# A graph network's edge sorting: paired one-hots, a maximum in pieces, ranks by column, and x transposed later

## The chip, the cores and the metric

One core of one Trainium2 chip runs the kernel as one program. The time is in device microseconds (us), the median of several executions. The engines are PE (TensorE, its weight loads shown apart as PEld), DVE (VectorE), ACT (ScalarE), POOL (GpSimd) and SP (SyncE, which here only starts DMAs). SBUF is the memory beside the engines, PSUM the one that PE writes.

## What is computed

A graph network with 3 layers on 3125 nodes of 128 features and 100,000 edges with 16 features each:

```python
s2 = concatenate([src, dst]); d2 = concatenate([dst, src]); ef2 = concatenate([ef, ef], axis=0)
h_prev = nf
for l in range(3):
    e_in = concatenate([h_prev[s2], h_prev[d2], ef2], axis=-1)
    msg = leaky_relu(e_in @ We1[l]) @ We2[l]
    red = segment_sum(msg, d2, num_segments=N)
    out = leaky_relu(concatenate([h_prev, red], axis=-1) @ Wn1[l]) @ Wn2[l]
    h_prev = out + h_prev
# result: _layernorm(x + out)
```

## The kernel before, in words

Nodes lie in 25 blocks of 128 (`NB`). An edge goes into one of 650 buckets by the blocks of its lower and its higher end, and a bucket's edges fill whole tiles of 128, so that in the layers every gather and every sum of a tile is a product with a one-hot matrix against one block. The kernel first sorts the edges into `records` in DRAM (up to about 1140 us), then builds tables and reads the records back (to about 1220 us), then runs the three layers. The change lies in the first two.

The 128 x 784 edges are worked on by column: 28 groups (`GROUPS`) of 28 columns (`GROUP`), each group in 4 chains of 7 columns (`CHAINS`, `RUN`).

- **Preparation** (DVE, L893 to L913). When all seven constants and both edge lists have landed: lower and higher end (L896, L897), their block numbers `lo_b` and `hi_b` (L898, L899), the places inside the block with a mark for padding, `loc` (L900 to L905), `ident16`, `zeros`, `ones`, and the bucket number `key` with two f16 copies (L911 to L913). PE transposes these (L1300), ACT copies them out (L739), and SP writes them to `rows_d` (L513), from where they come back as rows spread over all partitions, `hrow` and `krow` (L523, L528).
- **Counting** (DVE L940 and L927, PE L1311 and L1313, ACT L746). For each group DVE makes one-hots of the higher block (128 x 896, f16) and of the lower block (128 x 700, f16), comparing int32 block numbers with `iota`. PE multiplies them, once for each of 7 steps into one of two banks that ACT copies out to `cols` in four instructions of 32 partitions, and once more to add them up in `gath`.
- **Maximum** (DVE L945). The greatest absolute edge feature, one reduction over 128 x 12544; POOL then takes it across partitions (L658), and a scale of the features follows (L972 to L975).
- **First slots** (DVE L950 to L969). Totals, bucket sizes by a product on PE (L1330, L1332), tile numbers by a scan. Beside the maximum, PE transposes x (L1322) and ACT copies it to `hT` (L754).
- **The loop over groups** (DVE L1004 to L1059). `chain_bases` (L978 to L998) makes the starts of each bucket for a group; PE takes them to the edges (L1340). DVE then ranks each edge among the 128 of its column: equality of `krow` with the key (L1017), times a triangle of ones in PSUM, `tri_ps` (L1020), summed (L1023, into `within`). L1026 and L1032 pick the base, L1039 to L1053 make the record's row number `rowi`, L1056 the low half of the record, and `rec_set` is raised. Before the ranks of a group, `chain_bases` of the next one is done. `rec` and `rowi` are double: `rowi` of a group waits for the scatters of the group two before, `moved[h]`.
- **Scatter** (POOL L673). For each of the 28 columns of a group, one indirect DMA puts 128 records into place, 784 in all. Before the first, POOL waits until the whole of `records` is filled with blanks: two small DMAs of its own (L662) and two large ones of SP (L507), which repeat a block `blank` of 8 records of 68 bytes per partition, 544 bytes in one run.
- **Behind the loop** DVE finds out which tile belongs to which bucket (L1061 to L1090), clears buffers (L1091 to L1095), takes the maximum of `hT` (L1098), absolute weights (L1101), norms and scales (L1105 to L1122); PE and ACT make the first tables (L1353, L804) from `hT`; then PE transposes the records read back (L1407).

All of it runs on five queues in the written order; semaphores are the only ties between them. Inside the ranking and `chain_bases` several operands had been copied to PSUM beforehand (L758 to L761, L771), so that those DVE instructions have only one tensor in SBUF.

## Time and profile before

| | us |
|---|---|
| median of 3 executions | 3580.88 |
| lowest, highest | 3576.39, 3668.85 |
| the profiled execution | 3580.29 |
| its span in the profile | 3578.6 |
| POOL busy with scatters | 751.5 |
| DVE busy | 2741.3 (77%) |
| PE busy | 2436.7 (68%) |

The span reaches from the first to the last instruction that the profile shows; the profiled execution's own time lies 1.7 us above it. Times in the rows are counted from the span's start. The busy share of an engine says little here: the sorting at the beginning and the layers behind it have different limits.

### The profile page before, as it was taken

Reading aid. Unit: us, or ns where it says so; the run is one execution under the profiler, and the core shown is the slowest. Engines: PE = TensorE matmul, PEld = TensorE weight load, DVE = VectorE, ACT = ScalarE, POOL = GpSimd, SP = SyncE. Lnnn points to the kernel's source line nnn. Section 1 sums busy time; section 2 is a strip of 40 time slices with the busy share of each in tenths; the row PEclk is TensorE's granted clock in tenths of the full one; section 3 lists DMA queues with packets and bytes.
Section 4 is the critical chain, followed back from the end, with each engine's and each line's share of the span. In section 5 each row is a group of like instructions: output and inputs, shape, how many; then the busy total and the mean of one; then the engine's idle time right before and its main releaser. Section 6 shows DMA issues by size and latency. Waiting matters only on the chain.

```text
span 3578.6 us, 80654 instructions
## 1 busy us (share of the span) xinstructions
PE 2436.7 (68%) x26761; PEld 2103.2 (59%) x26762; DVE 2741.3 (77%) x3385; ACT 2062.6 (58%) x4138; POOL 800.0 (22%) x870
## 2 busy tenths in 40 slices
PE   5000000000004899999999999999999999999996
PEld 4000000000003678788787788888888788888885
DVE  8956565656564799999999877777777777777776
ACT  4000000000001678788777688888888688888885
POOL 0477777777775100000000100000000100000000
PEclk9555555555556899999999999999999999999998
DMA  8111111111112777777777455555555355555553
GB/s 251 46 45 33 45 37 41 34 44 37 39 22 71 234 257 248 253 254 250 248 257 246 174 193 192 193 192 194 195 195 195 107 195 195 195 193 193 191 193 123
DMA packets 227347, 563.67 MB, mean 158 GB/s; under 512 B 43272, under 2 KB 124238, under 8 KB 227182
## 3 DMA queue, kind: packets, MB, share of 16 engines
q1 hardware_dynamic: 199758, 547.80, 44.7%
q0 software_dynamic: 27552, 15.37, 2.3%
q8 instruction: 24, 0.39, 0.0%
q14 instruction: 13, 0.11, 0.0%
HBM read 413.11 MB, written 150.16 MB: 157 GB/s over the span
## 4 chain that ended last, share of the span: by engine, by line
PE 50%; POOL 19%; DVE 15%; issue 13%; DMA 1%; SPq 1%; ACT 1%; DVEq 0%; another core or an unknown queue 0%; ACTq 0%; POOLq 0%
POOL records L673 19%; PE gath L1454 18%; PE sums L1516 14%; PE sums L1454 9%; PE gath L1447 5%; DVE loop_buf L1200 3%; DVE big L1180 3%; PE sums L1447 2%; DVE loop_buf L1217 2%; DVE gsel L1184 2%; DVE table L1138 1%; DVE table L927 1%; PE sums L1537 1%; PE sums L1538 1%; DVE gsel L1064 0%
## 5 line engine op out<-in xcount | busy, mean ns | idle before, releaser
L1180 DVE SCALAR_TENSOR_TENSOR big<-big 128x768 f32<-128x768 f32 (+1 forms) x957 | 908.2, 949 | 360.2 <-ACT big L843 333.9
L1454 PE MATMUL gath<-table,gsel 128*128 x7488 | 1073.6, 273 | 0.0
L1200 DVE TENSOR_TENSOR loop_buf<-big,loop_buf 128x768 f16<-128x768 f32 x936 | 889.9, 951 | 0.0
L673 POOL DMA_INDIRECT records<-rec,rowi x784 | 751.5, 959 | 284.5 <-issue 247.3
L1516 PE MATMUL sums<-loop_buf 128*128 128x128 f16 x11232 | 781.2, 219 | 18.7 <-issue 15.8
L1454 PEld LDWEIGHTS gath<-table,gsel 128*128 128x128 f16 x7488 | 733.1, 98 | 84.0
L847 ACT ACTIVATE loop_buf<-big 128x768 f16<-128x768 f32 x936 | 782.4, 836 | 0.0
L843 ACT ACTIVATE big<-gath 128x512 f32<-128x512 f32 x936 | 560.0, 598 | 269.7 <-PE gath L1454 269.7
L1516 PEld LDWEIGHTS sums<-loop_buf 128*128 128x128 f16 x11232 | 647.0, 98 | 113.8 <-ACT sums L841 38.9
L1340 PE MATMUL sums<-table,fchunk 128*128 128x200 f16 x196 | 37.1, 365 | 877.2 <-DVE found L1032 864.7
L1454 PE MATMUL sums<-table,gsel 128*128 x3744 | 562.4, 273 | 14.6 <-DVE gsel L1184 14.6
L1340 PEld LDWEIGHTS sums<-table,fchunk 128*128 128x128 f16 x196 | 24.7, 136 | 889.3 <-issue 886.9
L783 ACT ACTIVATE rec<-big,sc_ef 128x448 f16 x28 | 18.7, 668 | 881.1 <-DMA records<-rec,rowi 881.1
L1447 PE MATMUL gath<-wst,fchunk 128*128 128x256 f16 x1872 | 510.9, 273 | 0.0
L838 ACT ACTIVATE big<-sums 128x256 f32<-128x256 f32 x936 | 353.4, 378 | 75.5 <-PE sums L1454 73.2
L1454 PEld LDWEIGHTS sums<-table,gsel 128*128 128x128 f16 x3744 | 361.2, 98 | 60.4 <-DVE gsel L1184 28.9
L841 ACT ACTIVATE sums<-iota 128x256 f32<-128x256 f16 x936 | 362.9, 388 | 30.3
L708 POOL TENSOR_SCALAR wcs<-wts,sc_w 128x128 f32<-128x128 f32 x2 | 1.2, 611 | 1573.1 <-DVE sc_w L1122 1573.1
L1447 PE MATMUL sums<-wst,fchunk 128*128 128x256 f16 x936 | 255.6, 273 | 21.0 <-issue 21.0
L1053 DVE SCALAR_TENSOR_TENSOR rowi<-rowb,rowc 128x28 int32<-128x28 int32 x28 | 5.3, 188 | 326.3 <-DMA records<-rec,rowi 326.0
L1447 PEld LDWEIGHTS gath<-wst,fchunk 128*128 128x128 f16 x1872 | 183.0, 98 | 31.7
L1217 DVE TENSOR_TENSOR loop_buf<-numc,iota 128x768 f16<-128x768 f16 x312 | 171.9, 551 | 3.9 <-DMA ssel_d<-loop_buf 0.3
(196 smaller groups left out, 1655.6 us busy)
## 6 DMA issues: line engine op xcount, KB each, us to landing
gsel<-gsel_d SPq DMA_DIRECT2D x208, 576.0 KB, 3.7
loop_buf<-ssel_d SPq DMA_DIRECT2D x208, 576.0 KB, 5.1
numb<-nums_d SPq DMA_DIRECT2D x106, 576.0 KB, 4.7
gsel_d<-gsel SPq DMA_DIRECT2D x104, 576.0 KB, 5.5
ssel_d<-loop_buf SPq DMA_DIRECT2D x104, 576.0 KB, 6.5
fchunk<-feat_d SPq DMA_DIRECT2D x630, 80.0 KB, 4.5
loop_buf<-rows_d SPq DMA_DIRECT2D x28, 896.0 KB
records<-rec,rowi POOLq DMA_INDIRECT x784
```

Source lines behind the costliest of these rows:

```text
L673: pool.indirect_dma_start(out=records[:, :], out_offset=bass.IndirectOffsetOnAxis(ap=rowi[:, h, g:g + 1].bitcast(U32), axis=0), in_=rec[:, ...
L838: act.activation(msg[:, place, 0:2 * D], gath6, ACT.Copy).then_inc(x6_set, 1)
L841: act.activation(gath6, iota[:, 0:2 * D], ACT.Copy, scale=0.0).then_inc(gath6_free, 1)
L843: act.activation(msg[:, place, 2 * D:MSG], gath[:, :], ACT.Copy).then_inc(x_set, 1)
L847: act.activation(m_hi[:, (q - 1) % RING, :], msg[:, (q - 1) % RING, :], ACT.Copy)\
L1180: return dve.scalar_tensor_tensor(m, m, SLOPE, m, ALU.mult, ALU.max)
L1184: dve.tensor_scalar(gsel[:, h, :], numb[:, h, :], part[:, 0:1], None, ALU.is_equal).then_inc(gsel_set[h], DMA)
L1200: dve.tensor_tensor(m_lo[:, place, :], msg[:, place, :], m_hi[:, place, :], ALU.subtract)\
L1217: last = dve.tensor_tensor(ssel[:, t % SLOTS:t % SLOTS + STEP, :, :].rearrange("p t s (e w) -> p (t s) e w", w=2), numc[:, 2 * t:2 * (t + ...
L1447: pe.matmul(uv, fchunk[:, p % PARTS, pair * P:(pair + 1) * P], wst[:, side, :, :].rearrange("p s f -> p (s f)"), start=fresh, stop=False, ...
L1454: return pe.matmul(uv, gsel[:, h, (2 * tc + s) * P:(2 * tc + s + 1) * P], at[n], start=False, stop=n == 3, skip_group_check=True)
L1516: last = pe.matmul(sum_at[i, s], m[:, place, w0:w0 + D], ssel[:, ts, s, :], start=False, stop=False, skip_group_check=True)
```

## The change

- **Order of loads.** The edge lists are loaded before the constants; DVE waits for the constants only behind `key`.
- **Preparation.** The ends, the shifts and `key` stay on DVE (5 instructions). POOL makes `zeros`, `ones` and `loc`, the latter in nine instructions on 784 elements each; ACT makes `ident16`, the f16 copies, and `lo_pairs` and `hi_pairs`, the block numbers as f16, each written twice side by side, `hi_pairs` with its columns in the order in which PE takes them.
- **Counting.** Both one-hots compare such pairs with pairs of `iota`; the lower one is made 26 wide (728 elements). PE reads its operands with strides accordingly.
- **Maximum.** It is taken in 16 pieces of 784 elements, one behind each of the last 16 groups' one-hots; across partitions by a product of `ones` with a scaled identity on PE and a reduction, in place of POOL's instruction.
- **Ranks.** `count_within` works on one column at a time: one instruction compares 128 elements of `krow` with a key per partition, multiplies by the triangle and accumulates; 28 of them per group. The triangle is now read from SBUF (`tri`), and the key is a scalar in SBUF; the output goes over `krow` as before.
- **Order in the loop.** The bases and ranks of the first group are made ahead of the loop, those of each next group behind `rec_set` of the one before.
- **x.** SP loads it when the last ranks are done (`krow_free`), PE transposes it behind the last `rec_set`, in four banks in turn, and ACT copies it to `hT`. DVE waits for PE (`hT_ps`) before it clears `loop_buf`, and for ACT (`hT_in`) before L1098.
- **Rows.** `load_rows` starts a group's four loads of `hrow` and its one of `krow` together; the first two groups' come ahead of SP's loop, the others when both buffers are free.
- **Blanks.** `blank` lies in a part of `recc` and has 64 records per partition; SP's blanking DMAs write runs of 3264 and 4352 bytes and come behind the rows of the first two groups.

```diff
+        hi_pairs, lo_pairs = (words_at(COLS, 2 * GROUP * NB + GROUP * NB + k * COLS).bitcast(F16).rearrange("p (j w) -> p j w", w=2)
+                              for k in range(2))
...
+        blank = recc[:, 2:4, :, :, :].rearrange("p k h t f -> p (k h t) f")
...
-            sp.dma_start(x0, x.rearrange("(b p) f -> p b f", p=P)).then_inc(s_x, 16)
-            sp.wait_ge(blank_set, 2)
-            for c0, c1 in ((2, CHUNKS // 2), (CHUNKS // 2, CHUNKS)):
-                sp.dma_start(records[c0 * CHUNK * P:c1 * CHUNK * P, :].rearrange("(c p t) f -> p c (t f)", p=P, t=CHUNK),
-                             blank[:, :, :].rearrange("p t f -> p (t f)").unsqueeze(1)
-                             .to_broadcast([P, c1 - c0, CHUNK * RW])).then_inc(blanked, 16)
...
+            for h in range(2):
+                load_rows(h * GROUP, h)
+            sp.wait_ge(blank_set, 2)
+            for r0, t, c in ((2 * CHUNK, 6 * CHUNK, 1), (8 * CHUNK, 8 * CHUNK, TILES // (8 * CHUNK) - 1)):
+                sp.dma_start(records[r0 * P:(r0 + t * c) * P, :].rearrange("(c p t) f -> p c (t f)", p=P, t=t),
+                             blank[:, 0:t, :].rearrange("p t f -> p (t f)").unsqueeze(1)
+                             .to_broadcast([P, c, t * RW])).then_inc(blanked, 16)
+            with sp.Fori(1, GTURNS) as it:
                 for h in range(2):
                     sp.wait_ge(hrow_free, it * 2 + h - 1 + KROW_AHEAD)
                     sp.wait_ge(krow_free, it * 2 + h - 1 + KROW_AHEAD)
                     sp.sem_inc(sp_go, 1)
-
+                    load_rows((it * 2 + h) * GROUP, h)
+
+            sp.wait_ge(krow_free, GROUPS + KROW_AHEAD)
+            sp.dma_start(x0, x.rearrange("(b p) f -> p b f", p=P)).then_inc(s_x, 16)
...
+            pool.memset(zeros[:, :], 0.0).then_inc(consts_set, 1)
+            pool.memset(ones[:, :], 1.0).then_inc(consts_set, 1)
+
+            pool.wait_ge(dve_seq, SHIFT_STEP)
+            for s, numbers in enumerate((lo_n, hi_n)):
+                pool.tensor_scalar(loc[:, :, s], numbers[:, :], 1.0, None, ALU.mult).then_inc(loc_seq, 1)
+            for s, blocks in enumerate((lo_b, hi_b)):
+                pool.wait_ge(loc_seq, 2 + 2 * s)
+                pool.tensor_scalar(dead, blocks, float(-P), None, ALU.mult).then_inc(loc_seq, 1)
+                pool.wait_ge(loc_seq, 3 + 2 * s)
+                pool.tensor_tensor(loc[:, :, s], loc[:, :, s], dead, ALU.add).then_inc(loc_seq, 1)
+            pool.wait_ge(loc_seq, 6)
+            pool.tensor_scalar(dead, hi_b, float(NB), float(-DEAD), ALU.is_equal, ALU.mult).then_inc(loc_seq, 1)
+            pool.wait_ge(loc_seq, 7)
+            for s in range(2):
+                pool.tensor_tensor(loc[:, :, s], loc[:, :, s], dead, ALU.add).then_inc(loc_seq, 1)
...
-            pool.partition_all_reduce(efmax[:, 1:2], efmax[:, 0:1], P, bass.bass_isa.ReduceOp.max).then_inc(efmax_all, 1)
...
+            act.wait_ge(s_const, 16 * 7)
+            act.activation(ident16[:, :], ident[:, :], ACT.Copy).then_inc(key16_set, 1)
+            act.wait_ge(dve_seq, SHIFT_STEP - 1)
+            act.activation(lo_pairs, lo_b.unsqueeze(2).to_broadcast([P, COLS, 2]), ACT.Copy).then_inc(pairs_set, 1)
+            act.wait_ge(dve_seq, SHIFT_STEP)
+            for r in range(CHAINS):
+                act.activation(hi_pairs.rearrange("p (g q r) w -> p r g q w", q=RUN, r=CHAINS)[:, r],
+                               hi_b.rearrange("p (g r q) -> p r g q", r=CHAINS, q=RUN)[:, r].unsqueeze(3)
+                               .to_broadcast([P, GROUPS, RUN, 2]), ACT.Copy).then_inc(pairs_set, 1)
+            act.activation(hib16, hi_b, ACT.Copy).then_inc(key16_set, 1)
+            act.wait_ge(dve_seq, KEY_STEP)
+            act.activation(key16, key[:, :], ACT.Copy).then_inc(key16_set, 1)
+            act.wait_ge(loc_seq, 2)
...
-            dve.wait_ge(s_const, 16 * 7)
             dve.wait_ge(s_edges, 32)
             then(dve.tensor_tensor(lo_n[:, :], src_t[:, :], dst_t[:, :], ALU.min))
             then(dve.tensor_tensor(hi_n[:, :], src_t[:, :], dst_t[:, :], ALU.max))
             then(dve.tensor_scalar(lo_b, lo_n[:, :], 7, None, ALU.logical_shift_right))
             then(dve.tensor_scalar(hi_b, hi_n[:, :], 7, None, ALU.logical_shift_right))
-            then(dve.tensor_scalar(src_t[:, :], lo_n[:, :], P - 1, None, ALU.bitwise_and))
-            then(dve.tensor_scalar(dst_t[:, :], hi_n[:, :], P - 1, None, ALU.bitwise_and))
-
-            then(dve.tensor_scalar(key[:, :], hi_b, float(NB), float(-DEAD), ALU.is_equal, ALU.mult))
-            then(dve.tensor_tensor(loc[:, :, 0], src_t[:, :], key[:, :], ALU.add))
-            then(dve.tensor_tensor(loc[:, :, 1], dst_t[:, :], key[:, :], ALU.add))
-            then(dve.tensor_copy(ident16[:, :], ident[:, :]))
-            then(dve.memset(zeros[:, :], 0.0))
-            then(dve.memset(ones[:, :], 1.0))
-            assert steps[0] == LOC_STEP
-
+            assert steps[0] == SHIFT_STEP
             then(dve.scalar_tensor_tensor(key[:, :], hi_b, float(NB), lo_b, ALU.mult, ALU.add))
-            then(dve.tensor_copy(key16, key[:, :]))
-            then(dve.tensor_copy(hib16, hi_b))
             assert steps[0] == KEY_STEP
+            dve.wait_ge(s_const, 16 * 7)
...
+            def hot_pairs(out, pairs, group, width):
+
+                dims = [P, GROUP, width // 2, 2]
+                return dve.tensor_tensor(out.rearrange("p j (a w) -> p j a w", w=2),
+                                         pairs[:, ds(group * GROUP, GROUP), :].unsqueeze(2).to_broadcast(dims),
+                                         iota[:, 0:width].rearrange("p (a w) -> p a w", w=2).unsqueeze(1).to_broadcast(dims),
+                                         ALU.is_equal)
+
+            dve.wait_ge(pairs_set, 1 + CHAINS)
+            def hot_group(group, h):
+
+                dve.wait_ge(hist_done, group - 1 + HIST_AHEAD)
+                hot_pairs(hot_hi[:, h, :, :], hi_pairs, group, HW)
+                hot_pairs(hot_lo[:, h, :, :], lo_pairs, group, LW).then_inc(hist_hot_set, 1)
+
+            with dve.Fori(0, GTURNS - EF // 2) as it:
                 for h in range(2):
-
-                    dve.wait_ge(hist_done, it * 2 + h - 1 + HIST_AHEAD)
-                    dve.tensor_tensor(hot_hi[:, h, :, :].rearrange("p q (r a) -> p q r a", a=HW), by_run(hi_b, it * 2 + h, HW),
-                                      numbers(HW), ALU.is_equal)
-                    hot_lo_of(hot_lo[:, h, :, :], it * 2 + h).then_inc(hist_hot_set, 1)
-
+                    hot_group(it * 2 + h, h)
             dve.wait_ge(s_ef, 16)
-            dve.tensor_reduce(efmax[:, 0:1], ef_t, AX_X, ALU.max, apply_absolute_value=True).then_inc(efmax_ready, 1)
+            with dve.Fori(GTURNS - EF // 2, GTURNS) as it:
+                for h in range(2):
+                    hot_group(it * 2 + h, h)
+                    f = nc.s_assert_within(it * 2 + (h - 2 * GTURNS + EF), 0, EF - 1,
+                                           skip_runtime_bounds_check_because="the last EF groups")
+                    dve.tensor_reduce(ef_most[:, ds(f, 1)], ef_t[:, ds(f * COLS, COLS)], AX_X, ALU.max,
+                                      apply_absolute_value=True)
...
+            def count_within(group, turn, h):
+
+                dve.tensor_copy(keyg, key[:, ds(group * GROUP, GROUP)]).then_inc(keyg_set, 1)
+                dve.wait_ge(krow_in[h], turn * 16 + 16)
+                dve.wait_ge(keyg_set, group + 1)
+                for j in range(GROUP):
+                    keys = krow[:, h, j * P:(j + 1) * P]
+                    last = dve.scalar_tensor_tensor(keys, keys, keyg[:, j:j + 1], tri[:, 1, :], ALU.is_equal, ALU.mult,
+                                                    accum_out=within[:, j:j + 1])
+                last.then_inc(krow_free, 1)
+
+            count_within(0, 0, 0)
+            dve.wait_ge(consts_set, 2)
+            dve.tensor_reduce(efmax[:, 0:1], ef_most[:, :], AX_X, ALU.max).then_inc(efmax_ready, 1)
+            dve.wait_ge(efmax_ready, 1)
+            dve.tensor_scalar(wcs[:, :], ident[:, :], efmax[:, 0:1], None, ALU.mult).then_inc(efd_set, 1)
...
+            then(dve.tensor_reduce(efmax[:, 1:2], bank(6)[:, 0:P], AX_X, ALU.max))
...
-                    keys = krow[:, h, :].rearrange("p (j e) -> p j e", e=P)
-                    dve.wait_ge(krow_in[h], it * 16 + 16)
-                    dve.tensor_tensor(keys, keys, key_ps[:, ds(group * GROUP, GROUP)].unsqueeze(2).to_broadcast([P, GROUP, P]),
-                                      ALU.is_equal).then_inc(same_set, 1)
-                    dve.wait_ge(same_set, group + 1)
-                    dve.tensor_tensor(keys, keys, tri_ps.unsqueeze(1).to_broadcast([P, GROUP, P]), ALU.mult)\
-                       .then_inc(before_set, 1)
-                    dve.wait_ge(before_set, group + 1)
-                    dve.tensor_reduce(within[:, :], keys, AX_X, ALU.add).then_inc(krow_free, 1)
...
+                    if h == 0:
+                        chain_bases(it * 2 + 1, it, 1)
+                        count_within(it * 2 + 1, it, 1)
+                    else:
+                        with dve.If(it < GTURNS - 1):
+                            after = nc.s_assert_within(it + 1, 1, GTURNS - 1,
+                                                       skip_runtime_bounds_check_because="not the last turn")
+                            chain_bases(after * 2, after, 0)
+                            count_within(after * 2, after, 0)
...
-            pe.wait_ge(s_x, 16)
             pe.wait_ge(cols_set, GROUPS + COLS_AHEAD)
             pe.wait_ge(rowsT_set, 1)
-            pe.sem_inc(pe_go, 1)
-            for b in range(NB):
-                last = pe.transpose(sums[:, b * P:(b + 1) * P], x0[:, b, :], ident[:, :])
-                if b % 4 == 3 or b == NB - 1:
-                    last.then_inc(hT_ps, 1)
-
-            pe.wait_ge(hT_in, BANKS)
...
+            pe.wait_ge(efd_set, 1)
+            pe.matmul(bank(6)[:, 0:P], ones[:, :], wcs[:, :], start=True, stop=True).then_inc(efmax_all, 1)
...
+            pe.wait_ge(s_x, 16)
+            pe.sem_inc(pe_go, 1)
+            for n in range(BANKS):
+                if n >= XT_BANKS:
+                    pe.wait_ge(hT_in, n + 1 - XT_BANKS)
+                for b in range(4 * n, min(4 * n + 4, NB)):
+                    last = pe.transpose(xT_bank(n)[:, b % 4 * P:(b % 4 + 1) * P], x0[:, b, :], ident[:, :])
+                last.then_inc(hT_ps, 1)
```

## Rows read from the trace of the kernel before

**Rows 1.** Groups of POOL: count, busy us, mean ns, idle us before, releasers.

```profile
L673 POOL DMA_INDIRECT records<-rec,rowi x784 | 751.5, 959 | 284.5 <-issue 247.3 <-DVE rec L1056 37.1
...
L716 POOL TENSOR_TENSOR wst<-wcs,wch 32x256 f16<-32x256 f32 x4 | 2.7, 668 | 0.3
...
L708 POOL TENSOR_SCALAR wcs<-wts,sc_w 128x128 f32<-128x128 f32 x2 | 1.2, 611 | 1573.1 <-DVE sc_w L1122 1573.1
```

**Rows 2.** Timeline of DVE inside the scatters: start us, us, instruction, idle before.

```profile
394.83 0.27 DVE L1039 SCALAR_TENSOR_TENSOR slot_i<-found,within 128x28 int32<-128x28 f32 x1
...
432.12 0.19 DVE L1048 SCALAR_TENSOR_TENSOR rowc<-rowa,slot_i 128x28 int32<-128x28 int32 x1
444.99 0.19 DVE L1053 SCALAR_TENSOR_TENSOR rowi<-rowb,rowc 128x28 int32<-128x28 int32 x1 [12.68 <-DMA records<-rec,rowi]
```

**Rows 3.** Timeline of DVE at the end of the scatters.

```profile
1051.61 0.19 DVE L1053 SCALAR_TENSOR_TENSOR rowi<-rowb,rowc 128x28 int32<-128x28 int32 x1 [17.37 <-DMA records<-rec,rowi]
...
1054.67 0.89 DVE L1064 SCALAR_TENSOR_TENSOR gsel<-sums,tiles_c,loop_buf 128x650 f32<-128x650 f32 x1
...
1055.61 0.89 DVE L1064 SCALAR_TENSOR_TENSOR gsel<-sums,tiles_c,loop_buf 128x650 f32<-128x650 f32 x1
...
1095.75 3.49 DVE L1098 TENSOR_REDUCE mx<-hT 128x1 f32<-128x3200 f32 x1
1099.15 1.75 DVE L1101 SCALAR_TENSOR_TENSOR big<-wts 128x1536 f32<-128x1536 f32 x1
1100.82 0.28 DVE L1103 TENSOR_SCALAR big<-ident,mx 128x128 f32<-128x128 f32 x1
```

**Rows 4.** Timeline of ACT and PE behind the last scatter.

```profile
1129.23 2.42 ACT L804 ACTIVATE table<-sums,sc 128x512 f16<-128x512 f32 x4 [7.73 <-remote]
...
1141.99 1.25 PE L1407 MATMUL sums<-ident,recc 128*68 128x128 f16 x10 [5.07 <-issue]
```

**Rows 5.** Timeline of DVE up to the first scatter.

```profile
10.52 0.97 DVE L896 TENSOR_TENSOR table<-table 128x784 int32<-128x784 int32 x1 [10.52 <-DMA below<-c_below]
...
21.78 1.09 DVE L940 TENSOR_TENSOR table<-table,iota 128x896 f16<-128x896 f16 x1
...
23.59 1.09 DVE L940 TENSOR_TENSOR table<-table,iota 128x896 f16<-128x896 f16 x1
...
72.19 13.21 DVE L945 TENSOR_REDUCE efmax<-big 128x1 f32<-128x12544 f32 x1
...
89.90 0.90 DVE L960 TENSOR_SCALAR table<-sums 128x325 int32<-128x325 f32 x2 [2.90 <-PE sums L1332]
...
102.07 0.57 DVE L982 TENSOR_TENSOR_SCAN sums<-gath,numb 128x200 f32<-128x200 f32 x1
...
106.75 3.88 DVE L1017 TENSOR_TENSOR loop_buf<-loop_buf,sums 128x3584 f16<-128x3584 f16 x1
```

**Rows 6.** Timeline of ACT at the start of the counting.

```profile
22.92 1.73 ACT L739 ACTIVATE fchunk<-sums 112x896 f16<-112x896 f16 x2 [20.17 <-PE sums L1300]
...
27.04 1.26 ACT L746 ACTIVATE table<-sums 32x175 f32 x4 [0.53 <-PE gath L1313]
```

**Rows 7.** One of the page's costliest groups: a one-hot of the first layer.

```profile
L1217 DVE TENSOR_TENSOR loop_buf<-numc,iota 128x768 f16<-128x768 f16 x312 | 171.9, 551 | 3.9 <-DMA ssel_d<-loop_buf 0.3
```

**Rows 8.** Timeline of POOL: the first scatter, and three near the end.

```profile
124.38 1.08 POOL L673 DMA_INDIRECT records<-rec,rowi  x1 [37.15 <-DVE rec L1056]
...
1098.77 0.96 POOL L673 DMA_INDIRECT records<-rec,rowi  x1 [0.30 <-issue]
1100.03 1.70 POOL L673 DMA_INDIRECT records<-rec,rowi  x1 [0.31 <-issue]
```

**Rows 9.** Timeline of PE: the first product of the bases.

```profile
102.30 1.32 PE L1340 MATMUL sums<-table,fchunk 128*128 128x200 f16 x7 [12.44 <-DVE table L994]
```

**Rows 10.** DMA issues up to 130 us: issues, KB each, median us to landing.

```profile
big<-ef SPq DMA_DIRECT2D x1, 6272.0 KB, 20.3
...
records<-blank SPq DMA_DIRECT2D x1, 4760.0 KB, 41.2
```

More of the change, by code:

```diff
@@ L257, in build @@
         rec = sb("rec", [P, 2, GROUP, RW], F16)
-        blank = sb("blank", [P, CHUNK, RW], F16)
         recc = sb("recc", [P, SLOTS_IN, PREP, CHUNK, RW], F16)
         hrow = recc[:, :, :, :, :].rearrange("p k h t f -> p (k h t f)")[:, 0:2 * RUN * P].rearrange("p (h e) -> p h e", h=2)
+        ef_most = sb("ef_most", [P, EF], F32)
+        blank = recc[:, 2:4, :, :, :].rearrange("p k h t f -> p (k h t) f")
+        assert SLOTS_IN == 4 and 2 * RUN * P <= 2 * BATCH * RW // P * P
         num16 = sb("num16", [P, 2, 2 * BATCH], F16)
@@ L357, in build @@
         consts_ps = sem("consts_ps")
-        key_in_ps = sem("key_in_ps")
+        pairs_set = sem("pairs_set")
+        consts_set = sem("consts_set")
+        key16_set = sem("key16_set")
+        loc_seq = sem("loc_seq")
+        efd_set = sem("efd_set")
+        keyg_set = sem("keyg_set")
         rec_set = sem("rec_set")
@@ L736, in _ @@
             act.sem_inc(cols_set, COLS_AHEAD)
+            act.wait_ge(s_const, 16 * 7)
[3 more added lines that the diff above has]
+            act.wait_ge(dve_seq, SHIFT_STEP)
+            for r in range(CHAINS):
+                act.activation(hi_pairs.rearrange("p (g q r) w -> p r g q w", q=RUN, r=CHAINS)[:, r],
[5 more added lines that the diff above has]
+            act.wait_ge(loc_seq, 2)
             act.wait_ge(rowsT_ps, 1)
@@ L750, in _ @@
                     last.then_inc(cols_set, 1)
-            for n in range(BANKS):
-                w = WIDE[n][1]
-                act.wait_ge(hT_ps, n + 1)
-                act.activation(hT[:, n * BANK:n * BANK + w], sums[:, n * BANK:n * BANK + w], ACT.Copy).then_inc(hT_in, 1)
             act.wait_ge(expand_set, 1)
@@ L769, in _ @@
                 line_of(h, h)
[L770 to L771 removed]
             act.wait_ge(scef_ready, 1)
[L773 removed]
+            act.wait_ge(loc_seq, 9)
             with act.Fori(0, GTURNS) as it:
@@ L804, in tables @@
                     act.activation(ab_table(s, 0), ab_bank(s), ACT.Copy, scale=sc[:, 0:1]).then_inc(thi_set, 1)
+            for n in range(BANKS):
+                w = WIDE[n][1]
+                act.wait_ge(hT_ps, n + 1)
+                act.activation(hT[:, n * BANK:n * BANK + w], xT_bank(n)[:, 0:w], ACT.Copy).then_inc(hT_in, 1)
             act.wait_ge(w2t_ps, 1)
@@ L1006, in _ @@
                     group = it * 2 + h
-                    if h == 0:
-                        chain_bases(it * 2 + 1, it, 1)
-                    else:
-                        with dve.If(it < GTURNS - 1):
-                            after = nc.s_assert_within(it + 1, 1, GTURNS - 1,
-                                                       skip_runtime_bounds_check_because="not the last turn")
-                            chain_bases(after * 2, after, 0)
-                    keys = krow[:, h, :].rearrange("p (j e) -> p j e", e=P)
-                    dve.wait_ge(krow_in[h], it * 16 + 16)
-                    dve.tensor_tensor(keys, keys, key_ps[:, ds(group * GROUP, GROUP)].unsqueeze(2).to_broadcast([P, GROUP, P]),
-                                      ALU.is_equal).then_inc(same_set, 1)
-                    dve.wait_ge(same_set, group + 1)
-                    dve.tensor_tensor(keys, keys, tri_ps.unsqueeze(1).to_broadcast([P, GROUP, P]), ALU.mult)\
-                       .then_inc(before_set, 1)
-                    dve.wait_ge(before_set, group + 1)
-                    dve.tensor_reduce(within[:, :], keys, AX_X, ALU.add).then_inc(krow_free, 1)
                     dve.wait_ge(base_ps, group + 1)
@@ L1294, in _ @@
             pe.sem_inc(hist_done, HIST_AHEAD)
-            pe.wait_ge(s_const, 16 * 7)
-            pe.wait_ge(dve_seq, KEY_STEP)
-            pe.sem_inc(pe_go, 1)
-            for k, numbers in ((0, key16), (1, hib16)):
+            pe.wait_ge(consts_set, 2)
+            for k, numbers in ((1, hib16), (0, key16)):
+                pe.wait_ge(key16_set, 3 - k)
+                pe.sem_inc(pe_go, 1)
                 for t in range(ROW_PARTS):
@@ L1365, in _ @@
             pe.wait_ge(rec_set, GROUPS + AHEAD)
+            pe.wait_ge(s_x, 16)
+            pe.sem_inc(pe_go, 1)
+            for n in range(BANKS):
+                if n >= XT_BANKS:
[3 more added lines that the diff above has]
+                last.then_inc(hT_ps, 1)
             pe.wait_ge(w_in, W_DMAS * DMA)
```

56 lines of the change are left out of this document (27 added, 29 removed).

## The prediction

> **What bounds the kernel now.** First the groups of instructions on POOL: 784 scatters of 959 ns stand in front of everything, and nearly all idle time between them is POOL's own issue, 247 us; only once, for 37.1 us, did it wait for DVE [rows 1]. Their starts lie 1.263 us apart, so 28 (a group) take 35.4 us, and the phase runs from 124.38 for 751.5 + 247.3 us to 1123.2. Then DVE's timeline inside that phase: its work for one group ends at 432.3, and its next instruction starts at 444.99, held 12.68 us by the scatters of two groups before [rows 2]. So in the loop DVE has 13 us to spare per group, and what it saves there is worth nothing; what makes POOL's scatters longer counts in full. Last, the end of the phase: the last group's index work on DVE waits for POOL at 1051.6 [rows 3], and from there a chain of tile map, norms and tables runs beside the last two groups to PE's transposes at 1141.99, 19 us after the last scatter [rows 4]. It hangs on the scatters by a fixed distance. Two things therefore move the time: when the first scatter starts (124.38), and how long 784 of them take. Everything behind 1142 is the same code, 2437 us of the 3578.6.
>
> **Part 1: up to the first scatter.** Before, DVE started at 10.52, the constants' landing, and made its first counting one-hot at 21.78 [rows 5]. Now the edges are loaded first; nine POOL instructions make `loc`, three DVE instructions of 1 us and five short ones leave DVE, and ACT fills the pairs. The constants still land at 10.5. ACT then writes 128 + 1568 + 4 x 392 elements; at the 175-element evictions' price (309 ns, four in 1.26 [rows 6]) and about 0.9 ns an element that is 0.25 + 1.5 + 2.5 = 4.3 us, so pairs stand at 15, `hib16` and `key16` (0.7 each) at 16.3. PE's 14 transposes end 1.1 behind, two copies of 1.73 together [rows 6] bring ACT to 19.4, and the first count eviction ends at 20.8, where it was 26.5 before (the second one's 27.04, less one turn of 1.80, plus 1.26).
>
> Counting: before, two DVE one-hots at 1x set a pitch of 1.81 us (21.78 to 23.59), 28 of them 50.4 us; then the feature maximum, 13.21 us in one piece [rows 5]. The paired form exists in the kernel already: 768 f16 elements in 551 ns [rows 7], which is 400 ns of stream at two elements a cycle and 151 ns around it; overlapped by 85 ns with its neighbour the pitches become 0.53 for 896 elements and 0.45 for 728, 0.98 us together. Next to it ACT's four evictions take 1.26 us and were idle 0.53 of each turn [rows 6]; with the hand-over I take 1.4 as the new pitch. A piece of the maximum is 13.21 / 16 = 0.83 plus 0.05. So 12 groups at 1.4 bring PE to 36.2 (DVE is two groups ahead, at 34.2), then 16 at 0.98 + 0.88 = 1.86 are 29.8: DVE is through at 64.0, PE at 64.7, where before the maximum ended at 85.4. If the pairs ran at 1x the pitch would stay 1.8 and 2.7 and 17 us of this part would be gone (a twentieth chance, since [rows 7] is the same form).
>
> From there to the scatter: 39.0 us before, 85.4 to 124.38 [rows 5, 8]. Gone: PE's 2.90 us wait, since the ranks of group 0 cover it, and one of the two `chain_bases` (102.07 to 106.75, 4.68). Added: 1.65 for the product of PE (1.32 busy [rows 9]), which the second `chain_bases` had hidden, and 1.2 for the maximum's reduce, scaling and read back. The ranks were 11.64 us in three passes of 3.88; now they are 28 times a 128-element pass with an accumulator. The map's 650-element ones have a pitch of 0.94 [rows 3]; less 522 elements at 1.04 ns that is 0.40, less the wait between dependent ones 0.37: 28 x 0.37 = 10.4 us, bounds 0.30 (8.4) and 0.50 (14). Sum 39.0 - 2.9 - 4.7 + 1.65 + 1.2 - 1.2 = 33.1, so the first scatter is at 64.7 + 33.1 = 97.8, 26.6 us earlier.
>
> What could be late: `loc` on POOL. A 128-element scalar op is 611 ns, a 256-element two-input op 668 ns [rows 1]: if all of it is fixed, nine ops cost 6 us, if all is per element 27; I take 18, done at 27, the 2176-element blank at 29. ACT needs `loc` only when the feature scale stands, behind 85. The blanking then starts behind the row loads, about 35; before, its second half landed 41.2 us after its issue, with the features (20.3 us) in front of it [rows 10], so 77 at the latest, now with rows eight times as long and nothing in front. POOL would have to take 6 us per op to make it the last. The pairs and POOL's ops meet for about 10 us while ACT sets the pace; I charge 3 us for it (0 to 10). Part 1: -24 us, range -29 to -10.
>
> **Part 2: the 784 scatters.** The ranks were formed with one operand in PSUM (`tri_ps`); now each of the 28 passes reads two tensors from SBUF, while POOL scatters. Of the 784 scatters only one behind the first two is above 0.98 us: the one at 1100.03 lasted 1.70 [rows 8]. Beside it DVE ran its only large instruction with two SBUF tensors, 1.75 us from 1099.15 on [rows 3]; the scatter before, begun at 1098.77, was at work when that one began and kept its 0.96 us. So a scatter that starts while such an instruction streams is held until it is over, 0.74 us here, and one that has started is not. How long POOL itself holds on: `slot_i`, 28 elements and two SBUF inputs, took 0.27 us where it started 0.03 before a scatter [rows 2], and 0.21 where it started 0.08 or more behind one. The read at a scatter's start is thus short.
>
> The Trainium skill, "SBUF — State Buffer", section "Who interferes with whom", says that a Vector instruction with two SBUF inputs contends with a GpSimd instruction that reads SBUF, and that whoever comes second is blocked for the whole of the other. The trace agrees for the scatter behind, not for the reverse: the 1.75 us instruction was as long as its elements make it although a scatter was running.
>
> Price: the passes of a group last 10.4 us, so 8.2 of its 28 scatters start among them, 221 in the 27 groups whose ranks are formed during scatters. A pass streams 0.133 us of 0.37 and lasts 0.28 at most. Held by the stream alone: 36% meet it, 0.067 mean, 5 us in all. Held for its whole duration: 76%, 0.14 mean, 24 us. I take 8, nearer to the first, since the 1.70 us scatter fits a release at the end of the stream (1100.8). Below nothing it can't be: POOL's pace never falls under 1.26 in this trace.
>
> **Part 3: moves with no price.** `chain_bases` and the ranks behind `rec_set` only change their order in DVE's 20 us, in front of 13 us of slack. x is loaded and transposed behind the last ranks: 25 transposes on PE with 7 copies on ACT beside them start at 1054, when DVE begins its map, and DVE needs `hT` at 1095.75 [rows 3]; even at 1 us a transpose they would be through at 1080. Before, they lay beside the maximum, so their leaving frees nothing by itself. SP's queue loses its first x load and gets rows earlier; its later waits are the same. The chain to 1142 keeps its length, but holds an ACT idle of 7.73 us that no engine of this core ended [rows 4]; it may fall elsewhere: 0, give or take 8.
>
> **Sum.** The profiled execution is 3580.3 us (span 3578.6), the median 3580.9. 3580.9 - 24 + 8 = 3565 us.
>
> **Rivals.** A, the other side: every scatter among the passes is held for a whole pass, or behind several. At 24 us / 221 = 0.11 us each the gain is used up; at 0.28 the loop grows by 62 us: 3580.9 - 24 + 62 = 3619. Were POOL shut out of a whole burst, 27 x 10.4 = 281 us: 3838. For it: the row of 0.74 us. Against the worst: behind the large instruction another DVE one follows at once (1100.82), and the scatter still went on.
> B: no hold at all, as a pass is short and its accumulator read leaves gaps: 3581 - 27 = 3554. For it: the map's 18 passes (one input in PSUM) lengthened no scatter.
> C: the opening gives back half: POOL's ops and the pairs shut each other out (7 us more than charged), ACT's strided copies are twice as long (2.5), a pass is 0.50 (3.6): 3565 + 13 = 3578.
> D: the pairs don't run at two elements a cycle: 12 x 1.82 + 16 x 2.70 = 65 us of DVE from 15.9 on, through at 81 instead of 64: 3565 + 17 = 3582.
>
> **How the numbers follow.** Forecast 0.60; A 0.17, of which 0.04 for bursts shut out; B 0.13; C and D 0.10. Without the worst of A and the best of B the range is 3546 to 3602. Two per cent is 72 us, about what a measurement of this kernel can tell from no change; the whole opening is 124 us and can't give 72, so faster by that 0.01, slower 0.05 (A's upper half), within 0.94.
>
> **What would show it.** Right: first scatter near 98; ACT back to back in the first 12 counting groups; one-hots of 0.61 and 0.53 us; a few scatters per group of 1.0 to 1.25 us, none outside the passes; 35.6 to 35.9 us a group. Wrong: groups of 36.5 us or more (A), 35.4 (B), `loc` or blanking released last before the first scatter (C), one-hots of 1.09 us (D), DVE no longer idle before `rowi`, or a tail behind the last scatter other than 19 us.

## The result: 3752.09 us against 3581.22, a ratio of 1.048, and the profile after

The changed kernel took 3752.09 us (four runs, 3749.01 to 3753.68), the kernel before 3581.22 beside it: a ratio of 1.048 with an interval of 1.046 to 1.050, where the forecast was 3565 and the range ended at 3602. (On chips like this one some runs of the kernel before take 3664 to 3672 us, 7 of 20 in all, where on the other kind of chip, told apart below, none of 67 was above 3576; they are left out of the ratios.) The profiled execution has a span of 3750.9 us, 172.3 more than before.

The opening went as forecast. DVE's timeline there, and POOL's first and last scatter:

```profile
13.42 1.07 DVE L969 TENSOR_TENSOR table<-table,iota 128x896 f16<-128x896 f16 x2 [3.09 <-ACT table L775]
...
59.67 0.53 DVE L969 TENSOR_TENSOR table<-table,iota 128x728 f16<-128x728 f16 x1
...
65.69 0.96 DVE L990 TENSOR_REDUCE ef_most<-big  x1
...
69.56 0.35 DVE L1011 SCALAR_TENSOR_TENSOR loop_buf<-loop_buf,gsel,tri 128x128 f16<-128x128 f16 x1 [0.54 <-DVE gsel L1006]
69.84 0.08 DVE L1011 DVE_READ_ACCUMULATOR loop_buf<-loop_buf,gsel,tri 128x1 f32 x1
69.84 0.35 DVE L1011 SCALAR_TENSOR_TENSOR loop_buf<-loop_buf,gsel,tri 128x128 f16<-128x128 f16 x1
```

One-hots of 0.53 us are the paired form at two elements a cycle, the last piece of the maximum ends at 66.65 (forecast 64.0), and the passes follow each other in steps of 0.27 us (forecast 0.37). The first scatter starts at 97.70 where 97.8 was forecast and 124.38 was before [rows 8].

The loss starts behind it. From the groups of POOL and DVE (count, busy, mean ns, idle before, releasers):

```profile
L705 POOL DMA_INDIRECT records<-rec,rowi x784 | 759.6, 969 | 477.7 <-issue 243.2 <-DVE rec L1100 234.5
```

```profile
L1011 DVE SCALAR_TENSOR_TENSOR loop_buf<-loop_buf,gsel,tri 128x128 f16<-128x128 f16 x784 | 242.9, 349 | 321.6 <-issue 314.9 <-DVE gsel L1006 4.9
...
L1011 DVE DVE_READ_ACCUMULATOR loop_buf<-loop_buf,gsel,tri 128x1 f32 x784 | 63.8, 81 | 254.4 <-issue 253.9
```

The scatters themselves take 8.1 us more than the 751.5 before [rows 1]: the forecast's part 2. But POOL now waits 234.5 us for DVE, 63.5 of it ahead of the first scatter and 171.0 in 13 waits of 12 to 14 us, one in every second group. And DVE, whose passes are busy for 243 + 64 us, stood idle for 569 us in front of them with "issue" as the reason: nothing the profile shows held it. How that looks, in DVE's timeline of one group:

```profile
463.20 0.35 DVE L1011 SCALAR_TENSOR_TENSOR loop_buf<-loop_buf,gsel,tri 128x128 f16<-128x128 f16 x1
463.47 0.08 DVE L1011 DVE_READ_ACCUMULATOR loop_buf<-loop_buf,gsel,tri 128x1 f32 x1
...
466.04 0.35 DVE L1011 SCALAR_TENSOR_TENSOR loop_buf<-loop_buf,gsel,tri 128x128 f16<-128x128 f16 x1 [1.31 <-issue]
467.44 0.08 DVE L1011 DVE_READ_ACCUMULATOR loop_buf<-loop_buf,gsel,tri 128x1 f32 x1 [1.05 <-issue]
468.83 0.35 DVE L1011 SCALAR_TENSOR_TENSOR loop_buf<-loop_buf,gsel,tri 128x128 f16<-128x128 f16 x1 [1.31 <-issue]
469.55 0.08 DVE L1011 DVE_READ_ACCUMULATOR loop_buf<-loop_buf,gsel,tri 128x1 f32 x1 [0.36 <-issue]
...
512.24 0.08 DVE L1011 DVE_READ_ACCUMULATOR loop_buf<-loop_buf,gsel,tri 128x1 f32 x1 [0.35 <-issue]
512.24 0.35 DVE L1011 SCALAR_TENSOR_TENSOR loop_buf<-loop_buf,gsel,tri 128x128 f16<-128x128 f16 x1
512.94 0.08 DVE L1011 DVE_READ_ACCUMULATOR loop_buf<-loop_buf,gsel,tri 128x1 f32 x1 [0.35 <-issue]
512.95 0.35 DVE L1011 SCALAR_TENSOR_TENSOR loop_buf<-loop_buf,gsel,tri 128x128 f16<-128x128 f16 x1
```

```profile
505.89 0.95 POOL L705 DMA_INDIRECT records<-rec,rowi  x1 [0.31 <-issue]
520.75 0.95 POOL L705 DMA_INDIRECT records<-rec,rowi  x1 [13.91 <-DVE rec L1100]
```

After some instructions in steps of 0.27 us the rest come one by one at multiples of 0.70 us, mostly 1.40, an 0.08 us read too. Some 4 us after POOL has ended its last scatter (begun at 505.89), two come every 0.70 us. So the engine isn't slow, its instructions start late. In the other group of each turn the passes run at 0.27, with at most two late steps. The late stretch begins at the same place of the loop's code in every turn: behind the 7th or 8th of the 56 instructions of the ranks in the second half (the 11th in the first turn), in e18 and e20 below as well.

What the late instructions wait for the profile doesn't show. The two DMA queues that it marks as "instruction" moved 39 packets over the whole span, and none between 180 and 1220 us, while the loop ran late turn after turn; in e18, e20 and e5 it is the same. So these queues don't fetch the loop's code anew each turn.

The balance of the 172.3 us: first scatter -26.7; from the first to the last scatter's start 1172.8 us against 997.9, +175.0; from there to PE's first transposes of the records 38.5 against 19.8, +18.8; behind them +5.2. The third term looks like the same thing, in the map's small instructions and in ACT's copies of hT, which show releasers that aren't of this core (timeline of ACT in the tail, beside the 7.73 of [rows 4]); e11 below, nearly the same program without late instructions, takes 7.1 us there:

```profile
1235.54 0.60 ACT L847 ACTIVATE hT<-sums 128x512 f32<-128x512 f32 x1 [9.24 <-remote]
...
1277.63 0.49 ACT L851 ACTIVATE w<-gath 128x384 f32<-128x384 f32 x1 [12.18 <-remote]
```

### The profile page after: what moved, and what is told of

It is laid out like the page before. It is cut to its first block, busy times and chain, and to the rows that moved or that the text cites. A ratio compares the mean times of both kernels' runs of the same rounds, so it can differ in the third digit from the quotient of the medians.

```text
span 3750.9 us, 82198 instructions
## 1 busy us (share of the span) xinstructions
PE 2433.7 (65%) x26763; PEld 2103.0 (56%) x26764; DVE 2666.0 (71%) x4905; ACT 2065.8 (55%) x4145; POOL 831.5 (22%) x880
## 4 chain that ended last, share of the span: by engine, by line
PE 49%; DVE 26%; issue 22%; ACT 1%; another core or an unknown queue 1%; DMA 1%; SPq 1%; DVEq 0%; ACTq 0%; POOL 0%
PE gath L1514 17%; PE sums L1576 13%; PE sums L1514 9%; DVE loop_buf L1011 7%; PE gath L1507 4%; DVE loop_buf L1256 3%; DVE big L1236 3%; PE sums L1507 2%; DVE loop_buf L1273 2%; DVE gsel L1240 2%; DVE table L1070 1%; DVE found L1076 1%; DVE fchunk L1047 1%; DVE table L957 1%
## 5 line engine op out<-in xcount | busy, mean ns | idle before, releaser
L705 POOL DMA_INDIRECT records<-rec,rowi x784 | 759.6, 969 | 477.7 <-issue 243.2
L1514 PE MATMUL sums<-table,gsel 128*128 x3744 | 563.5, 273 | 13.1 <-DVE gsel L1240 13.1
L1011 DVE SCALAR_TENSOR_TENSOR loop_buf<-loop_buf,gsel,tri 128x128 f16<-128x128 f16 x784 | 242.9, 349 | 321.6 <-issue 314.9
L805 ACT ACTIVATE numb<-table 128x175 f32 (+1 forms) x28 | 14.2, 510 | 782.7 <-DVE sums L1045 698.4
L1011 DVE DVE_READ_ACCUMULATOR loop_buf<-loop_buf,gsel,tri 128x1 f32 x784 | 63.8, 81 | 254.4 <-issue 253.9
```

The lines of the kernel that those rows point to most:

```text
L705: pool.indirect_dma_start(out=records[:, :], out_offset=bass.IndirectOffsetOnAxis(ap=rowi[:, h, g:g + 1].bitcast(U32), axis=0), in_=rec[:, ...
L1011: last = dve.scalar_tensor_tensor(keys, keys, keyg[:, j:j + 1], tri[:, 1, :], ALU.is_equal, ALU.mult, accum_out=within[:, j:j + 1])
L1514: return pe.matmul(uv, gsel[:, h, (2 * tc + s) * P:(2 * tc + s + 1) * P], at[n], start=False, stop=n == 3, skip_group_check=True)
```

## The experiments

**First set: supply, port or work.** Three theories: DVE's instructions are supplied too slowly once its loop has many (supply; in what follows the word says only that instructions start late with nothing in the profile to hold them); its passes and the scatters shut each other out at SBUF (port); DVE simply has more to do (work). Beside this set the kernel before took 3582.5 us.

e1, the ranks in three whole passes again, in the new order (the triangle of group 0 from SBUF, the keys copied to PSUM by ACT as before; lines shortened):

```
-                for j in range(GROUP):
-                    last = dve.scalar_tensor_tensor(keys, keys, keyg[:, j:j + 1], tri[:, 1, :], ALU.is_equal, ALU.mult, accum_out=...)
+                dve.tensor_tensor(keys, keys, key_ps[...], ALU.is_equal)
+                dve.tensor_tensor(keys, keys, triangle[...], ALU.mult)
+                dve.tensor_reduce(within[:, :], keys, AX_X, ALU.add)
```

> The changed kernel with the ranks in three whole passes as before (key and triangle in PSUM), all else as changed. Three theories for the 171 us. Supply: DVE's loop over groups, with 28 passes written out twice, is longer than what DVE can keep of its instructions, is fetched anew each turn and runs dry. Port: passes with two SBUF inputs and POOL's scatters hold each other. Work: DVE simply has more to do. All three: the scatters are back to 999 us without a wait for DVE; the first one starts at 97.7 plus some 4 us for the slower ranks of group 0, about 102. Total 3581 - 22 = 3559, within 3553 to 3566. Should it stay above 3600, the loss isn't in the ranks at all.

Measured 3650.7, ratio 1.020 (1.018 to 1.022). No theory allowed that: all three gave 3553 to 3566. POOL waits for DVE only once behind the first scatter (3.4 us), but 237 scatters last 0.98 us or more, most of them 1.1, 59 us in all, and the tail takes 41.7 us. SP starts late here too. Its instructions in front of a row load (duration ns: min/median/max), here and in the kernel before:

```profile
L530 SPq FUSED_REGOPS  x75: 5/698/1399, 300.3 to 1003.1; - x75
L530 SPq MOVE recc<-rows_d x75: 5/698/710, 302.4 to 1003.8; - x75
```

```profile
L523 SPq FUSED_REGOPS  x72: 55/55/55, 321.9 to 929.8; - x72
L523 SPq MOVE recc<-rows_d x72: 29/29/29, 322.0 to 929.9; - x72
```

A register operation of 55 ns takes 698 in the median: the same 0.70 us step on another engine. SP's loop is that of the changed kernel, where the median stays at 55 and the longest takes 711. So the whole-pass form lost too, and "DVE's loop is too long" wasn't all of it. Why the scatters are longer here, beside passes with one tensor in SBUF, stays open; e10 below, with the same DVE code and none of the lateness, has 11 such scatters.

e2, the passes kept, their triangle read from PSUM inside the loop (`tri[:, 1, :]` becomes `tri_ps`):

> The changed kernel with the triangle of the 28 passes read from PSUM inside the loop, so that each pass has one tensor in SBUF; the number of instructions is the same. Port: the 97 lengthened scatters (8.8 us) are gone, DVE's passes run without gaps, and the time falls to about 3560. Supply: the lengthened scatters are gone too, but DVE's gaps between instructions stay, a turn of two groups stays at 85 us, total 3740 to 3755. Work: as supply, but with no idle DVE.

Measured 3768.3, ratio 1.053 (1.050 to 1.055), 13 us above supply's range. Scatters of 0.98 us or more fell from 93 to 3; the waits for DVE stayed:

```profile
L705 POOL DMA_INDIRECT records<-rec,rowi x784 | 750.7, 957 | 498.0 <-DVE rec L1100 255.2 <-issue 242.2 <-remote 0.6
```

So the two-input passes do lengthen scatters, as part 2 said, but the loss stays without them. Port falls as its cause.

e3, the 28 passes as an inner loop of 4 by 7 (`with dve.Fori(0, 4)` around seven passes), so that DVE's body is short:

> The changed kernel with the 28 passes as an inner loop of 4 turns with 7 passes written out: the same passes with the same inputs, a quarter of the code. Supply: the gaps go, POOL no longer waits for DVE, lengthened scatters stay (5 to 15 us); first scatter 98 to 100, total 3555 to 3572. Port and work: nothing changes, 3740 to 3760 (the inner loop's branches add to DVE).

Measured 3830.0, ratio 1.070 (1.068 to 1.073): the worst. Neither range had it. Idle time of the passes with reason "issue" is 615 us, and POOL waits 5 us or more for 21 of the 27 groups behind the first. Fewer instructions in the program don't help.

e5, the kernel before with 54 memsets of one element per group on DVE, some 1 us of work (the 5 us expected below are too many) in front of 13 us of slack:

> The kernel before with 54 clearings of one element behind the ranks of every group, each some 0.1 us with no input at all: 5 us of work in 13 us of slack, but as many more instructions as the change wrote out. Supply: POOL comes to wait for DVE every second group, total 3680 to 3760. Port and work: 3581 as before, no wait of POOL.

Measured 3712.9, ratio 1.037 (1.035 to 1.040), with DVE's memsets 427.7 us idle for "issue". So late instructions alone bring such a loss, with every step of the kernel as before, and work falls too. That the loop's code is fetched anew each turn, supply's mechanism in e1's expectation, isn't borne out by the two instruction queues, as said above.

**Second to fourth set: small edits, all of them cures.** To find what in e1 slowed SP:

e8, the group loop as before (order, whole passes, a wait for each kind of load) with the new opening; e10, e1 with only SP's waits split (shortened):

```
 sp.wait_ge(hrow_free, ...)
-sp.wait_ge(krow_free, ...)
 sp.sem_inc(sp_go, 1)
 (four loads of hrow)
+sp.wait_ge(krow_free, ...)
+sp.sem_inc(sp_go, 1)
 (one load of krow)
```

> The changed kernel's opening and tail with the group loop put back as it was: three whole passes for the ranks (keys and triangle in PSUM), the next bases and the ranks ahead of the table product, the two kinds of row loads behind a wait each. DVE's loop body has 60 instructions in the listing, as in the kernel before (the changed kernel 114, e1_whole 62). If the length of DVE's loop body, or its order, is what costs: scatters of 0.96 us throughout as in the kernel before, SP's four loads in 1.9 us, the first scatter at 100 to 106, total 3557 to 3565. If something of the new opening (the blank inside the record buffers, the row loads ahead of the blanking) lengthens the scatters of e1_whole: over 200 scatters of 1.1 us again and 3610 to 3650.

> e1_whole with one edit: SP waits for the chain rows and for the key rows separately and issues each kind behind its own wait, as in the kernel before. DVE's loop body stays at 62 instructions in the new order. If the ten loads issued in one go are what lengthens the scatters of e1_whole: 3557 to 3570. If DVE's loop body (its length or its order) does it: 3640 to 3660 and SP's loads again slow (over 10 us for four).

e6, four memsets per group; e7, one scatter of 28:

> The kernel before with four memsets of one element added on DVE behind each group's ranks: about 0.4 us of work per group, 68 instructions in the loop body instead of 60. If a body a little longer than 60 already leaves what the chip holds: scatters lengthened and SP's four loads slow as in e1_whole, 3610 to 3660. If the limit lies higher, or e1_whole's loss has another cause: 3580 to 3586 and scatters of 0.96.

> The changed kernel with one of each group's 28 scatters (27 in 28 records are left out, so later sums lack them). Supply theory: without the scatters DVE's 28 passes come at 0.27 to 0.35 us also in the loop, and two groups take 40 to 55 us, the loop some 560 to 770 us instead of 1208. If the slow steps of 0.7 and 1.4 us stay without scatters, they have nothing to do with POOL: two groups take about 80 us still.

e8 3554.6, ratio 0.996 (0.995 to 0.997); e10 3548.7, 0.994 (0.992 to 0.996); e6 3572.0, 1.000. In e7, which leaves 27 of 28 scatters out, a group takes DVE 17.5 us with its passes in steps of 0.27 (3065 us in all). The kernel before took 3569.2 here, 12 us less than at first, and e8, e10 and e6 all lay below the lowest time expected for them, by 2 to 8 us: a first sign that something other than the edits had changed. It looked as if one SP wait were worth 100 us, so it was tried on the changed kernel itself (e11) and the other way round (e12), with twenty memsets (e13):

> The changed kernel with one edit: SP waits for the chain rows and for the key rows separately, and issues each kind behind its own wait (the edit that took e1_whole from 3651 to 3549). If the joint issue is the whole cause: the first scatter at 98, no waits of scatters for DVE, 3550 to 3562. If DVE's 56 passes and their accumulator reads per turn are enough by themselves: waits of 10 us and more for DVE in every second group stay, 3720 to 3755.

> The kernel before with one edit: SP waits for both kinds of row buffer and then issues all five loads. If the joint issue brings the slow steps whatever DVE's loop holds: SP's register operations at 0.7 us instead of 0.055, over 150 scatters of 1.1 us, 3640 to 3680. If it needs the changed order of DVE's loop too: 3569 to 3585 and scatters of 0.96.

> The kernel before with twenty one-element memsets on DVE per group (about 2 us of work): 100 instructions in the listing of its loop body; 60, 62 and 68 ran at full speed, 114 (changed kernel) and 168 didn't. If the number of short instructions counts in proportion: 54 of them cost 131 us, twenty cost some 30 to 50, 3600 to 3630. If there is a threshold above 100: 3570 to 3590. If a threshold below 100: waits of POOL for DVE as with 54, 3640 to 3720.

e11 3557.3, ratio 0.997 (0.996 to 0.998); e12 3567.2, 0.999; e13 3569.9, 1.000. The joint wait costs nothing in the old kernel, yet splitting it seemed to give 195 us in the new one. That called for a finer cut, the same number of instructions or another place for them (`sp.sem_inc(sp_go, 1)` once more per group, or eight times ahead of the loop):

> The changed kernel with SP's semaphore instruction behind the two waits given twice, so that SP's loop has exactly as many instructions as in e11_after_split, with the joint waits kept. If the joint waits are the cause: 3740 to 3760 and the slow steps as in the changed kernel. If the number of SP's instructions in the loop is: 3550 to 3565.

> The changed kernel with eight semaphore instructions of SP ahead of its loop of row loads; the loop itself is unchanged. If where SP's loop lies in its code decides: 3550 to 3565, or another loss than 5%. If the joint waits are the cause wherever the loop lies: 3740 to 3760.

> e11_after_split with the same eight instructions ahead of SP's loop. If the split waits cure it wherever the loop lies: 3552 to 3562. If the place decides: it can lose again, over 3600.

> The kernel before with 54 memsets per group on DVE (e5, +3.7%) and eight semaphore instructions of SP ahead of its loop of row loads. If the place of SP's loop decides: 3570 to 3600. If DVE's instructions do it by themselves: 3690 to 3720, as e5.

e14 3557.8, e15 3558.7 and e16 3559.1 (0.997 to 0.998), e17 3569.4 (1.000). Everything cured everything. An edit that changes next to nothing and always helps is a sign that the edit isn't what helps. Each set since the first had run on another chip, and the kernel before took 3567 to 3570 in them, not 3581.

**Fifth and sixth set: the control.** The changed kernel, unchanged, beside e11, unchanged:

> The changed kernel, unchanged, once more, beside e20. If the loss is the kernel's own (the order of SP's waits, or the place of its instructions): 3740 to 3760 also where the kernel before takes 3568. If the loss belongs to the chip or to its condition in the first sets: 3553 to 3562 where the kernel before takes 3568, and 3740 to 3760 only where it takes 3581 or 3668.

> e11_after_split, unchanged, on the same chip as e18. If SP's joint issue is the cause: 3552 to 3562 whatever e18 takes. If the chip's condition is: the same as e18 within 0.5%, at 3557 or at about 3750.

This chip gave 3580.4 for the kernel before, and 3749.3 for e18 (1.047, 1.045 to 1.049) and 3753.8 for e20 (1.049, 1.046 to 1.051). e20 is e11 to the last character, which took 3557.3 elsewhere. POOL's group in e11 and in e20:

```profile
L712 POOL DMA_INDIRECT records<-rec,rowi x784 | 766.2, 977 | 310.5 <-issue 246.5 <-DVE rec L1107 64.0
```

```profile
L712 POOL DMA_INDIRECT records<-rec,rowi x784 | 758.2, 967 | 486.0 <-issue 243.1 <-DVE rec L1107 242.9
```

and DVE's passes in them:

```profile
L1018 DVE SCALAR_TENSOR_TENSOR loop_buf<-loop_buf,gsel,tri 128x128 f16<-128x128 f16 x784 | 216.5, 353 | 3.3 <-DVE gsel L1013 0.5
```

```profile
L1018 DVE SCALAR_TENSOR_TENSOR loop_buf<-loop_buf,gsel,tri 128x128 f16<-128x128 f16 x784 | 243.7, 349 | 309.8 <-issue 301.1 <-DVE gsel L1013 4.7 <-remote 1.8
```

One program, 3.3 us of idle time in front of its passes on one chip and 309.8 on another. So the readings of the second to fourth sets show no cure; each compared a kernel on one chip with another kernel's loss on a different one. What can be said of SP's waits is said by e18 and e20, side by side on one chip: splitting them gave nothing back. On the place of instructions nothing was run where the loss occurs. e21 (e8 once more) was meant for a chip of the slow kind and met another of the fast kind:

> e8_old_order, unchanged. If the kernel before takes 3568 here: 3550 to 3560, as before, and nothing new. If it takes 3580 with single runs at 3668 (the chips on which the changed kernel took 3750): 3555 to 3570 if a group loop of the old length and order is what runs at full speed there, 3640 or more if anything of the new opening, or SP's loop, brings the slow steps there.

It took 3552.0, the kernel before 3567.0 (0.996, 0.994 to 0.998).

## Why the prediction was wrong

**What failed** is a step of part 3: the moves "only change their order in DVE's 20 us, in front of 13 us of slack", and with it the pass's price of 0.37 us in the loop. The 56 passes and 56 reads of a turn cost their work only where instructions arrive in time. On the prediction's chip two groups took 84.7 us in the changed kernel instead of 70.7 (medians over the turns; 84.7 in e18, 85.0 in e20), 175 us over the loop where part 2 and 3 together had 8. The other term of part 3 failed too: "the chain to 1142 keeps its length", at 0, give or take 8, measured +18.8. It doesn't hang on the scatters by a fixed distance: from the last scatter's start to the records' transposes it is 19.8 us in the kernel before, 38.5 in the changed one and 7.1 in e11 and e12. No rival had this mechanism. The sign given for A, groups of 36.5 us or more, came (42.4 in the mean) without A's cause, for the scatters took 8.1 us more and not 62.

**It could have been asked from the trace of before**, which came from such a chip. Its tail has the step of 0.70 us in the map's small instructions; the same stretch of the same DVE code in e12, on a chip of the fast kind, has none of it (from the last accumulator read ahead of the map's memsets to the first large memset behind it DVE takes 3.8 us, where the trace of before needs 18.0):

```profile
1082.21 0.19 DVE L1085 TENSOR_SCALAR map_t<-map_i 128x3 int32<-128x3 int32 x1 [0.34 <-DVE map_t L1085]
1083.61 0.17 DVE L1085 TENSOR_SCALAR map_t<-map_i 128x3 int32<-128x3 int32 x1 [1.20 <-DVE map_t L1085]
1084.32 0.17 DVE L1085 TENSOR_SCALAR map_t<-map_i 128x3 int32<-128x3 int32 x1 [0.54 <-issue]
```

```profile
1072.70 1.51 DVE L1084 TENSOR_SCALAR map_t<-map_i 128x3 int32<-128x3 int32 x6
1074.24 0.56 DVE L1087 TENSOR_TENSOR map_t<-map_t 128x3 int32<-128x3 int32 x3
```

The ACT idle of 7.73 us "that no engine of this core ended" [rows 4] was most likely the same mark; e12 has none there, and its records' transposes start at 1127.74, not 1141.99. The prediction saw it and gave it 8 us either way instead of asking what it would do to 112 small instructions per turn in place of 6 long ones. Of the 13.1 us between the spans of the kernel before and of e12, 12.7 are this tail.

**Part 1 was right**: -26.7 us measured, first scatter 97.70 for 97.8. That it came out to 0.1 us is luck, for its terms missed against each other (counting through 2.7 us late, the ranks 2.8 us shorter), and the 3 us charged on top for POOL and the pairs weren't needed. C and D fell.

**Part 2 was right in kind**: 93 scatters of 0.98 us or more, 8.7 us in all, for a forecast of 8. The match is luck: it holds with the passes strung out over 50 us in every second group. Where they come at full speed (e11) it is 159 scatters and 15.1 us, within the 0 to 24 given; e2 shows that the second SBUF input is the reason. The share was mis-sized: 153 of the 161 scatters that start during a pass of e11 are lengthened, where the forecast took a number near 36%, and each by about 0.10 us. On the Trainium skill's rule ("SBUF — State Buffer", section "Who interferes with whom"): the scatter that comes second is held, by 0.1 us here (the longest lasts 1.07 beside a pass) and not for a whole pass, and POOL, when it comes first, doesn't hold the passes: they keep their 0.35 us throughout.

**On the fast kind the changed kernel's nearest relatives came out as forecast.** e11 against e12, two profiled executions on one chip: first scatter 97.87 for 122.94 (-25.1), the scatters +14.0, the rest the same within 0.5, spans 3554.0 and 3565.5. The measured ratio 0.997 stands beside the forecast's 3565 / 3580.9 = 0.996. The changed kernel itself ran on no such chip; e11, e14 and e15 differ from it only in where SP waits or in some added semaphore instructions.

**A version faster than both on the fast kind**: e10, the new opening and order with whole passes, 0.994 where the changed kernel's relatives have 0.997, since its scatters aren't lengthened (754.3 us busy for 766.2 in e11). On the slow kind neither e8 nor e10 was run, and e1, e10's nearest, lost 2% there, so nothing is shown for that kind.

## What to carry to other kernels

An idle engine with "issue" or "remote" as its releaser in steps of one size, in front of instructions of any length, points to instructions that start late and not to the work or its data; before many short instructions replace a few long ones, look whether the trace of before has such steps anywhere, and price them in. And when small edits all cure, repeat the unchanged kernel beside one of them on one chip first: one control here was worth more than the eleven runs ahead of it.

## What the runs showed of the hardware

- Instructions can start late, at multiples of 0.70 us, on DVE and SP: while POOL scatters mostly one per 1.40 us, some 2 to 5 us after it has stopped two per 0.70 us. It goes with the chip: the traces of the first comparison, the first set and the fifth have it, the kernel before only in its tail; the other four sets have it nowhere. The six sets ran on six chips (that of the first comparison isn't on record), so whether it is the chip, its condition at the time or the place where a program was loaded stays open. The profile's two instruction queues moved nothing in the loop behind its first turn, on either kind, so what the instructions wait for is open too.
- How many short instructions it takes isn't settled: 54 memsets per group brought 131 us on a slow-kind chip, and the kernel before, with 6 long passes per turn, runs its loop without lateness there; four and twenty were tried on the fast kind alone, where even 54 cost nothing (e17: 0.1 us idle in front of 1512 of them). That e3's loops made it worse than straight code was measured, not explained.
- A pass of 128 f16 elements with an accumulator has a pitch of 0.27 us, its 0.08 us read hidden in the next pass.
